# A decoder layer on one core: V's tiles 4 to 7 projected alone behind 0 to 3, and a new order of K's stages on five engines

## The reference, cut to what matters

```python
def _dequant(codes, scales):                 # codes 0..15, one scale per 128 input rows
    w = codes.astype(jnp.float32) - 8.0
    return w * jnp.repeat(scales, GS, axis=0)
...
x = _layernorm(x)
q = x @ _dequant(q_codes, q_scales)          # 32 heads of 128
k = x @ _dequant(k_codes, k_scales)          # 8 heads of 128
v = x @ _dequant(v_codes, v_scales)          # 8 heads of 128
q = _rope(q)                                 # pairs turned by cos and sin of the position
k = _rope(k)
scores = q @ k.T * HD ** -0.5 + causal mask  # 4 heads of q share one of k and v
out = softmax(scores) @ v @ _dequant(o_codes, o_scales)
x = x + out
```

## Time and profile before

| | |
|---|---|
| median of 3 runs | 1104.31 us (1104.18 to 1104.64) |
| the profiled execution | 1104.83 us, with a span of 1103.0 us |
| PE busy | 1053.8 us, 96% of the span |
| DVE, POOL, ACT busy | 922.6 us (84%), 717.6 us (65%), 691.5 us (63%) |

### The profile page before, as it was taken

One profiled execution on the slowest core, in us unless ns is written; L12 is line 12 of the kernel. 1 busy time (PEld: TensorE's weight loads), 2 busy tenths in 40 slices (PEclk: granted clock), 3 DMA queues, 4 the chain that ended last, 5 costly groups with the idle time before them and its releaser, 6 DMA issues.

```text
span 1103.0 us, 18870 instructions
## 1 busy us (share of the span) xinstructions
PE 1053.8 (96%) x5406; PEld 507.8 (46%) x5416; DVE 922.6 (84%) x1738; ACT 691.5 (63%) x1499; POOL 717.6 (65%) x789
## 2 busy tenths in 40 slices
PE   5979999899999999999999999999999999889998
PEld 3434433444444444444444444544544554444443
DVE  7867887799888888888888889999999998988873
ACT  4536655766777777777777776666666666463320
POOL 4568667877767776776677677878878877332200
PEclk9989999999999999999999999999999999999999
DMA  9565220777767667666766676677777665532443
GB/s 340 192 153 163 86 83 15 148 150 166 144 153 163 148 141 159 157 142 148 158 159 134 154 161 141 144 155 161 148 154 160 153 131 121 110 118 53 100 96 86
DMA packets 309652, 155.74 MB, mean 141 GB/s; under 512 B 257712, under 2 KB 270256, under 8 KB 309584
## 3 DMA queue, kind: packets, MB, share of 16 engines
q1 hardware_dynamic: 301808, 141.56, 55.9%
q10 hardware_dynamic: 7776, 13.37, 4.3%
HBM read 89.07 MB, written 4.19 MB: 85 GB/s over the span
## 4 chain that ended last, share of the span: by engine, by line
PE 70%; DVE 5%; ACT 5%; issue 2%; ACTq 1%; POOL 0%; DMA 0%; DVEq 0%; SPq 0%; POOLq 0%
PE side_ps L712 9%; PE side_ps L878 9%; PE side_ps L714 9%; PE side_ps L713 9%; PE proj_ps L898 8%; PE out_ps L898 8%; PE proj_ps L1049 4%; PE score_ps L861 3%; PE score_ps L863 2%; PE score_ps L862 2%; PE proj_ps L1054 2%; PE score_ps L1020 2%; ACT prob L1224 1%; DVE x_acc L2011 1%; ACT w_b L1251 1%
## 5 line engine op out<-in xcount | busy, mean ns | idle before, releaser
L1570 POOL TENSOR_TENSOR w_b<-prob,w_b 128x896 f16<-128x896 f32 (+2 forms) x192 | 188.9, 999 | 29.3 <-ACT w_b L1251 29.0
L712 PE MATMUL side_ps<-hT,w_a 128*128 128x512 f16 x504 | 191.1, 379 | 1.5 <-DVE rot L1927 1.5
L714 PE MATMUL side_ps<-hT,w_a 128*128 128x512 f16 x504 | 191.0, 379 | 0.0
L713 PE MATMUL side_ps<-hT,w_a 128*128 128x512 f16 x504 | 191.0, 379 | 0.0
L1563 POOL TENSOR_SCALAR prob<-prob,row_inv 128x512 f32<-128x512 f32 (+3 forms) x256 | 171.0, 683 | 22.6 <-DVE row_inv L2084 17.2
L2011 DVE SCALAR_TENSOR_TENSOR x_acc<-proj_ps,o_now,x_acc 128x1024 f32<-128x1024 f32 x120 | 153.6, 1280 | 38.3 <-PE proj_ps L898 38.3
L1577 POOL TENSOR_TENSOR q_sb<-rot,q_sb 128x512 f16<-128x512 f32 x64 | 74.7, 1167 | 139.2 <-ACT q_sb L1216 139.2
L1224 ACT ACTIVATE prob<-score_ps,neg_max 128x512 f32<-128x512 f32 (+3 forms) x256 | 133.0, 522 | 48.3 <-DVE neg_max L1987 39.4
L2011 DVE SCALAR_TENSOR_TENSOR x_acc<-out_ps,o_now,x_acc 128x1024 f32<-128x1024 f32 x120 | 152.7, 1272 | 0.0
L898 PE MATMUL out_ps<-work,w_b 128*128 128x512 f16 x496 | 127.3, 379 | 2.0 <-DVE x_acc L2011 2.0
L898 PE MATMUL proj_ps<-work,w_b 128*128 128x512 f16 x496 | 127.3, 379 | 2.0 <-DVE x_acc L2011 1.1
(11 more groups left out here) (244 smaller groups left out, 2103.6 us busy)
## 6 DMA issues: line engine op xcount, KB each, us to landing
stage_c<-in_codes_dram SPq DMA_DIRECT2D x80, 256.0 KB, 2.9
stage_o<-in_codes_dram SPq DMA_DIRECT2D x64, 256.0 KB, 4.0
stage_s<-in_scales_dram SPq DMA_DIRECT2D x64, 256.0 KB, 3.8
ctx_raw<-in_ctx_dram ACTq DMA_DIRECT2D x32, 256.0 KB, 3.3
work<-w_b SPq DMA_TRANSPOSE x261, 3.0
x_acc<-in_x_dram SPq DMA_DIRECT2D x8, 512.0 KB, 9.4
k_sb<-in_codes_dram SPq DMA_DIRECT2D x16, 256.0 KB, 8.2
v_sb<-in_scales_dram SPq DMA_DIRECT2D x16, 256.0 KB, 9.0
```

Of the source, the lines that this page charges most:

```text
L712: pe.matmul(o, stat(0), mov(0), start=first, stop=False)
L713: pe.matmul(o, stat(0), mov(1), start=False, stop=False)
L714: return pe.matmul(o, stat(1), mov(0), start=False, stop=last)
L1570: ins = pool.tensor_tensor(prob16[:, 1, to:to + w], prob[:, at:at + w], prob16[:, 0, to:to + w], ALU.subtract)
```

## The change

It does four things, all ahead of the attention loop.

- **V's weights and tiles.** `V_ALONE` goes from 6 to 8: V's tiles 4 to 7 run alone, 6 and 7 behind the pair 4 and 5 and into banks of `side_ps` (`v_bank`). The second half of V's weights (pieces 8 to 15) is loaded ahead of the rows of tokens 4 to 7, and DVE and ACT take its steps ahead of those tokens' normalisation.
- **K's codes** get four places (`K_STAGES`), two of them in `stage_s`.
- **K's stages.** On DVE the sum of tile m - 1 stands behind all adds of tile m, and the eviction of V between them. On POOL the lower half of a tile moves from the end of its own stage to behind the join of the next tile. On ACT the swap and the upper half move likewise (`k_upper(x - 2)`), V's evictions behind K's, and an eviction of K waits for the swap of two tiles back.
- **PE and the end.** `BESIDE` loses V 6 and 7; its 64 blocks are spread over 15 K tiles; Q 0 and Q 1 stand last. They start by halves of their weights (`piece_done`), have their own places for the rotation (`q_rot`, `q_swap_of`), and are turned from K's tiles 13 and 15 on (`Q_TURN_AT`). The first scores wait for 9 of K's tiles instead of 15.

The diff, cut:

```diff
-V_ALONE = 6
+V_ALONE = 8
 V_STAGES = 8
+K_STAGES = 4
-BESIDE = ([("V", n) for n in range(V_ALONE, V_HERE - 1)] + [("Q", b) for b in range(B)] + [("V", V_HERE - 1)])
+BESIDE = [("V", n) for n in range(V_ALONE, V_HERE)] + [("Q", b) for b in range(B)]
...
-Q_PAIR = PAIRS - 3
+Q_TURN_AT = {PAIRS - 3: 0, PAIRS - 1: 1}
+Q_SUM_AT = PAIRS - 2
 def beside_from(n):
-    return n * len(BESIDE) // PAIRS
+    return min(n * len(BESIDE) * 2 // (2 * PAIRS - 2), len(BESIDE) * KB)
...
+        def k_codes_in(m):
+            return stage_c[:, m % 2, :] if m % K_STAGES < 2 else stage_s[:, m % 2, :].bitcast(I32)
...
         def v_bank(n):
-            return out_ps[:, n - 2, :] if n in (2, 3) else proj_ps[:, n % 2, :]
+            return (out_ps if n in (2, 3) else side_ps if n in (6, 7) else proj_ps)[:, n % 2, :]
...
             def load_k(m):
-                if m >= 2:
-                    sp.wait_ge(k_cut, m - 1)
+                if m >= K_STAGES:
+                    sp.wait_ge(k_cut, m - K_STAGES + 1)
...
             load_x(3)
+            for m in range(8, 16):
+                load_v(m)
             for t in range(TB, TT):
-                load_v(2 * t)
-                load_v(2 * t + 1)
                 load_x(t)
-            for m in range(4):
+            for m in range(K_STAGES):
                 load_k(m)
             turn_h(4)
             turn_h(5)
...
             for kb in range(KB):
                 for n in (4, 5):
                     v_group(n, kb)
+            for n in (6, 7):
+                for kb in range(KB):
+                    v_group(n, kb)
             for x in range(PAIRS):
...
-                        pe.wait_ge(k_ready, K_TILES - 1)
+                        pe.wait_ge(k_ready, NKV + 1)
...
                 if m >= 2:
                     act.wait_ge(*((k_cosed, k_joined)[kb], m - 1))
+                    act.wait_ge(k_swapped, m - 1)
...
             for x in range(PAIRS):
                 m = x
                 ahead = ABS_AT.get(x, ())
+                k_evict(m, 0)
+                k_evict(m, 1)
                 for n in v_over(x):
                     v_evict(n)
-                k_evict(m, 0)
...
-                k_evict(m, 1)
+                if x >= 2:
+                    k_upper(x - 2)
...
                 if x:
                     k_swap(m - 1)
...
-                if x:
-                    k_upper(m - 1)
...
-            for m in range(14):
+            for m in range(16):
                 v_lower(m)
-            k_convert(0)
-            k_convert(1)
-            v_lower(14)
-            v_lower(15)
+            for m in range(K_STAGES):
+                k_convert(m)
             h_lower(4)
             h_lower(5)
-            k_convert(2)
-            k_convert(3)
+            k_convert(K_STAGES)
+            k_convert(K_STAGES + 1)
             h_lower(6)
-            k_convert(4)
-            k_convert(5)
             h_lower(7)
...
             for x in range(PAIRS):
                 if x:
                     k_join(x - 1)
+                if x >= 2:
+                    k_lower(x - 2)
...
-                if x:
-                    k_lower(x - 1)
...
+            v_scale(13)
+            v_rest(2)
+            v_scale(14)
+            v_scale(15)
+            h_stats(4)
             h_stats(5)
-            v_rest(2)
-            row_roots(2, last_stats[0], 0, lambda: v_scale(12), H_UP)
+            row_roots(2, last_stats[0], 0, lambda: v_rest(3), H_UP)
             h_norm(4)
...
             for x in range(PAIRS):
                 m = x
+                k_add(m, 2, 3)
                 for n in v_over(x):
                     v_rest(n)
-                k_add(m, 2, 3, 4)
+                k_add(m, 4)
                 if x in Q_CUT_AT:
                     piece_scale(Q_CUT_AT[x], Q_CUT_AT[x] % 2)
-                if x < Q_PAIR + 2:
-                    if x:
-                        k_sum(m - 1)
-                    k_add(m, 5)
...
+                k_add(m, 5)
                 if x in Q_CUT_AT:
                     piece_lo(Q_CUT_AT[x], Q_CUT_AT[x] % 2, q_region(Q_CUT_AT[x]), Q_UP)
                 k_add(m, 6, 7)
...
+                if x:
+                    k_sum(m - 1)
```

More of the change, by code:

```diff
@@ L310, in k_part, with q_rot, q_swap_of @@
             return k_sb[:, m % NKV, l, m // NKV * S:(m // NKV + 1) * S]
+        def q_rot(p):
+            return work[:, p, 0:S] if known(p) and p < Q_AHEAD else rot[:, :]
+        def q_swap_of(p):
+            return work[:, p, S:2 * S] if known(p) and p < Q_AHEAD else swapped[:, :]
         late_swap, late_rot = (x_acc[:, 7, j * S:(j + 1) * S] for j in range(2))
@@ L597, in _ @@
             load_o(o_index(0, 0), 0)
-            for m in range(6, 2 * NKV):
+            for m in range(K_STAGES + 2, 2 * NKV):
                 load_k(m)
```

176 lines of the change are left out of this document (86 added, 90 removed).

## The result

The changed kernel takes **1096.95 us** (median of four runs, 1096.55 to 1098.01) against 1104.47 for the kernel before: a ratio of 0.9933, 95% interval 0.9915 to 0.9950. The forecast was 1089.7 in a range of 1084.5 to 1096.0. The sign was right, the size was not: 7.5 us were won where 14.6 were forecast.

A forecast was written before the change was run, and what follows sets the result against it. PE lost 22.3 us ahead of the first scores, all that could be won; expected remaining losses 0 + 3.5 + 2.5 + 1.7 = 7.7 gave a gain of 14.6, so 1104.3 - 14.6 = 1089.7 us, range 1084.5 to 1096.

The forecast's parts named there:

- V's weights: Ahead of K's tiles: weights ready in time, waits of 2.4 and 5.3 us go; all 13.5 us lost there won.
- Tokens 4-7 and the first codes: Ahead of K's tiles: tokens 4 and 5 done at 54, POOL's first join near 73, behind waits for K's codes.
- K tiles 1 to 5: PE stalls 1.1 us from tile 3's start, tiles 3 to 5 add 0.8 each; together 3.5, bounds 0.8 and 7.
- K tiles 9 to 12: DVE bounds at 6.9 us a tile against PE's 6.2; about 2 absorbed; loss 2.5, bounds 0.8 and 4.2.
- The end: Tile 15 to first scores: DVE's owed sums 2.4 us, then adds 4.0; loss 1.7, bounds 1.0 and 3.0.
- the sum keeps the join out in every tile: Rival, K's tiles: DVE's sum lengthens POOL's tile by 0.69 us, stall grows 2.8, 1092.5 us; chance 0.12.
- the old pace: Rival: K's tiles keep their measured paces, 6.7 to 7.75 us a tile; gain 9, 1095.3 us; chance 0.15.
- V's weights still late: Rival, V's tiles: a wait of 2 us and as much again at the halved clock, 1093.5 us; chance 0.05.
- the slower case: Rival: steps of successive K tiles no longer overlap, 9.9 us a tile, 34 us later, 1138 us; chance 0.03.
- Nothing stalls but the end: Rival, K's tiles: first codes come earlier than forecast, 1084.6 us; chance 0.12.
- The three middle terms: Middle values of losses in K tiles 1 to 5, K tiles 9 to 12 and the end: 3.5, 2.5, 1.7 us.
- Their worst sum: Worst ends up to first scores: 2 + 7 + 4.2 + 3 = 16.2 us lost, gain 6.1, 1098.2 us.

The follow-up runs named there:

- The run with filled cosines and sines: Changed kernel, but POOL fills the areas without input instead of computing cosine and sine products of K's tiles 9 to 12 (results wrong): 1092.67 us, ratio 0.9884.
- the fill on POOL: Changed kernel, but from K stage 6 POOL fills a scratch area, some 0.5 us, between a tile's sine and its next two-operand instruction: 1095.83 us, ratio 0.9918.

## Why the prediction was wrong, by its steps

**V's weights: right.** PE runs from 36 to 75 us without a pause, at full clock; K's tile 0 starts at 60.79 (61.0 forecast); the last lower half is done at 45.3 (42.5 to 48.0). All 13.5 us of the head went. The wait of 5.3 went with V 6's new bank. For the wait of 2.4 the prediction named loads and the order on DVE; the new order of the loads wasn't needed, so the other is left. As the run with V 6 and 7 beside K shows, little of this head counts by itself.

**Tokens 4-7 and the first codes: right in mechanism, 1.3 late.** Token tile 5's lower half ended at 54.34 (54 forecast), the next step took 11.5 (11), the last 8.5 (8): first join 74.31 (73). What the prediction did not draw from it is how far this join bounds what comes behind it: PE's ten microseconds of lead were a wait put somewhere else, as the run with V 6 and 7 beside K shows (first scores 0.1 us apart), and the run with the old orders (nothing won). The gain of 7.5 comes from the stretch behind the join: 109.1 us from the first join to the first scores before (72.90 to 182.02), 99.2 now, 94.4 by the forecast.

**K tiles 1 to 5: the step that failed most.** 3.5 were forecast, 6.6 came. The sum started with tile 3 (from what it calls tile 2's join, the second one, which turns tile 1) and put the wait in tile 2 at nothing. But PE already waited there, 2.7 us in three pauses, since the sum of tile 0 stands ahead of tile 2's adds on DVE, and the swap and cosine of tile 0 ahead of ACT's evictions of tile 2; the 1.3 us by which the first join came late fall into this wait too. The pace behind it, 6.95 a stage, was right (7.0), and so, nearly, was the rest of the term: 3.7 in tiles 4 to 6, of which 0.5 stands behind the sum of tile 4 that the join kept out. The codes sent early take 5.1 of the 6.6 us off.

**K tiles 9 to 12: 2.5 forecast, 3.8 measured** (on PE in tiles 10 to 13, since DVE is behind). That DVE is the bound was right: it is busy for 28.66 of 28.89 us. Two terms were mis-sized. A tile took (158.62 - 129.73) / 4 = 7.2, not 6.9, since beside POOL a piece's scaling takes 1.29 us on average (1.2 counted) and its lower half 0.99 (0.7 counted). And the 2 us that the ring and DVE's idle time were to absorb weren't: four tiles of 7.2 against PE's 6.2 give 4.0, and 3.8 came. The run with filled cosines and sines, where the two take 0.79 and 0.77, bears the cause out. The Trainium skill ("SBUF — State Buffer", section "Who interferes with whom") says that a Vector instruction with two SBUF inputs contends with a GpSimd instruction that reads SBUF, and that issue order decides who blocks; the rows at 117.82 and 135.72 agree, where POOL was first and DVE took 1.75 for 0.69 and 1.61 for 0.7.

**The end: 1.7 forecast, 3.1 measured.** PE starts tile 15 at 165.38. DVE at this place:

```profile
167.00 1.74 DVE L1813 TENSOR_TENSOR rot<-rot,swapped 128x512 f32<-128x512 f32 x1 [0.56 <-POOL swapped L1575]
168.67 0.68 DVE L1942 TENSOR_TENSOR work<-side_ps,work 128x512 f32<-128x512 f32 x1
169.27 1.39 DVE L1806 SCALAR_TENSOR_TENSOR x_acc<-score_ps,k_scale,x_acc 128x512 f32<-128x512 f32 x2
```

Tile 15's adds begin 3.9 us behind its start, where 2.4 were counted: the sum of tile 13 waits 0.56 for POOL's sine and is kept out for 1.05. The six adds then take 4.0, as counted. With sums that aren't kept out (the fill on POOL) 2.7 of the 3.1 remain. Behind the first scores, where nothing was counted, 0.5 us went (first scores 8.5 earlier, span 8.0).

The three terms together are 5.8 us short, of the 7.1 by which the gain was missed. Another 0.5 went behind the first scores, and the rest is the rounding of the stretches (0.3) and the difference between the two profiled executions and the medians (0.5).

**The rivals.** The first one, *the sum keeps the join out in every tile*, came mainly in the other direction: where POOL has no idle time it is the join that keeps the sum out, and DVE pays 1.05, not POOL 0.69; the price is about 1 us in all, not 2.8. The direction that it names is there too (the join at 140.61 takes 1.66), but POOL had been idle. The second, *the old pace*, was refuted in kind and in price: the pace did improve, and with the old one the time would have been 1106.3, not 1095.3, since it too overlooked the wait in the first tiles. *V's weights still late* (1093.7 by its own terms, not 1093.5) did not come, nor did the slower case. *Nothing stalls but the end* did not come either, and not even the early codes make it so: 1.4 us in tiles 2 to 6 and what is lost in tiles 10 to 13 remain.

**The range.** The three middle terms all came near their worst ends (6.6 of 7, 3.8 of 4.2, 3.1 of 3.0). Their worst sum, 1098.2, held the result; the range had been cut at 1096 as if only some of them could go wrong. No common cause is shown for them: the early codes take off the first and leave the other two, and the filled cosines and sines take off most of the second and 0.9 of the third. That the run with early codes and the fill comes to 1090.83, near the forecast, is luck in the terms: it loses 0.8, 3.8 and 2.7 us where 3.5, 2.5 and 1.7 were counted.

## What to carry to other kernels

A wait removed at the head is won only if the engine that bounds the next stretch starts earlier; follow that engine's first instruction, here one join, back to what releases it, and move that first (here four loads in a queue, 5.0 us). Where two engines keep each other out, count the bounding engine's instructions at the length that they have beside the other (here 1.29 and 0.99 us instead of 0.79 and 0.77), and see which one starts first where one releases the other. Keep the sum of the worst ends in the range unless a reason is given why the terms can't all go wrong: here three separate ones did.
